# Attention's first score steps placed between the last second layers of an expert stage, and the end of the kernel re-ordered

## The reference, cut to what matters

```
x = x + conv(norm(x))        # a long convolution over time, done with a Fourier transform
x = x + experts(norm(x))     # 8 experts, the best 2 of each token weighed by a softmax
x = x + attention(norm(x))   # 16 heads of 8 features, 4 sets of queries, causal softmax
x = x + experts(norm(x))     # the same 8 experts again
```

## Time and profile before

| | us |
|---|---|
| median of 3 runs | 831.67 |
| the three runs | 830.97, 831.67, 833.51 |
| the profiled execution's own time | 832.0 |
| its span | 830.3 |
| busy: PE, PEld | 778.1, 425.8 |
| busy: ACT, DVE, POOL | 717.3, 641.0, 552.9 |
| granted TensorE clock, mean | 0.994 of full |

### The profile page before, as it was taken

How to read it: one execution, slowest core, us unless ns; L and a number is a source line. 1 busy time by engine, 2 the same in 40 slices (tenths; PEclk the granted TensorE clock), 3 DMA queues, 4 the chain that set the end, 5 groups by cost and what they waited for, 6 DMA issues and landing times.

```text
span 830.3 us, 20345 instructions
## 1 busy us (share of the span) xinstructions
PE 778.1 (94%) x7697; PEld 425.8 (51%) x7697; DVE 641.0 (77%) x1914; ACT 717.3 (86%) x917; POOL 552.9 (67%) x610
## 2 busy tenths in 40 slices
PE   3898999999999899999999999999999999999995
PEld 1444766766667333333333333333334677777774
DVE  6896899977897656776776776777555999888884
ACT  4623988988988999999999999999998799999983
POOL 2785566455534889888888888889886454454442
PEclk9999999999999999999999999999999999999998
DMA  9211000000023234443433433334400000000000
GB/s 292 82 51 52 2 1 2 2 2 1 2 55 96 62 97 102 103 98 83 101 89 88 96 100 81 87 103 102 103 1 2 2 14 15 15 13 16 13 15 17
DMA packets 38521, 46.87 MB, mean 56 GB/s; under 512 B 6185, under 2 KB 23858, under 8 KB 38418
## 3 DMA queue, kind: packets, MB, share of 16 engines
q1 hardware_dynamic: 38418, 45.51, 20.9%
HBM read 28.71 MB, written 16.78 MB: 55 GB/s over the span
## 4 chain that ended last, share of the span: by engine, by line
PE 57%; ACT 13%; DVE 10%; POOL 8%; issue 8%; ACTq 0%; POOLq 0%; DVEq 0%
PE psum L944 16%; PE psum L890 14%; PE psum L1242 12%; ACT prob L1200 10%; PE psum L1191 5%; PE psum L1300 4%; DVE mixed L956 3%; POOL prob L1215 3%; DVE hidden_parts_first L913 2%; PE psum L674 2%; PE psum L1084 1%; PE psum L766 1%; POOL prob L1212 1%; POOL prob L1210 1%; POOL rstd L367 1%
## 5 line engine op out<-in xcount | busy, mean ns | idle before, releaser
L1200 ACT ACTIVATE prob<-psum 128x1536 f32<-128x1536 f32 x256 | 347.4, 1500 | 15.5 <-PE psum L1191 15.5
L1242 PE MATMUL psum<-prob,vstack 128*32 128x256 f32 (+1 forms) x2048 | 204.9, 495 | 1.6 <-DVE o_tok L1250 1.6
L890 PE MATMUL psum<-xt_parts,w_parts 128*128 128x512 f16 x768 | 186.6, 379 | 0.0
L956 DVE SCALAR_TENSOR_TENSOR mixed<-psum,comb_y,mixed 128x128 f32<-128x128 f32 x512 | 143.2, 340 | 2.1 <-PE psum L944 2.1
L920 POOL TENSOR_TENSOR hidden_parts_second<-hidden_second,hidden_parts_second 128x512 f16<-128x512 f32 x64 | 77.4, 1209 | 94.4 <-ACT hidden_parts_second L906 94.3
L920 POOL TENSOR_TENSOR hidden_parts_first<-hidden_first,hidden_parts_first 128x512 f16<-128x512 f32 x64 | 76.7, 1201 | 73.4 <-ACT hidden_parts_first L906 73.1
L1210 POOL TENSOR_SCALAR_AFFINE_SELECT prob<-prob 128x512 f32<-128x512 f32 x128 | 84.2, 658 | 44.5 <-ACT prob L1200 39.1
L1191 PE MATMUL psum<-qstack,kstack 32*128 32x512 f16 x768 | 99.6, 384 | 9.6 <-POOL prob L1215 4.8
L1191 PEld LDWEIGHTS psum<-qstack,kstack 32*128 32x128 f16 x768 | 24.8, 91 | 158.1 <-ACT prob L1200 139.6
L904 ACT ACTIVATE hidden_second<-psum,b 128x512 f32<-128x512 f32 x128 | 88.3, 690 | 20.2 <-PE psum L890 16.5
L890 PEld LDWEIGHTS psum<-xt_parts,w_parts 128*128 128x128 f16 x768 | 72.0, 99 | 64.3 <-issue 1.4
(11 more groups left out here) (137 smaller groups left out, 1018.1 us busy)
## 6 DMA issues: line engine op xcount, KB each, us to landing
qstack<-qk_parts SPq DMA_DIRECT2D x128, 128.0 KB, 3.6
qk_parts<-parts SPq DMA_DIRECT2D x64, 192.0 KB, 3.1
kstack<-qk_parts SPq DMA_DIRECT2D x128, 32.0 KB, 3.5
stream<-L_attn_a_u SPq DMA_DIRECT2D x4, 512.0 KB, 8.2
kept_x<-stream SPq DMA_DIRECT2D x4, 512.0 KB, 2.7
out<-mixed SPq DMA_DIRECT2D x8, 256.0 KB, 2.3
mirror<-u_mirror SPq DMA_DIRECT2D x4, 256.0 KB, 7.2
w_whole<-L_ffn_W SPq DMA_DIRECT2D x1, 1024.0 KB, 8.6
```

The source lines that it names most:

```text
L890: last = e.matmul(bank(u % 4), m.w1[:, w_part, ex, cols], xt_parts[:, s, x_part, :], start=(n == 0), stop=(n == len(PRODUCTS) - 1))
L956: last = e.scalar_tensor_tensor(out=m.y[:, t0 + t, :], in0=bank(down_bank(m, i))[:, t * P:(t + 1) * P], scalar=comb_y[:, s, t, ex:ex + 1], ...
L1200: e.activation(prob[:, n % PROBS, :], psum[:, TILE * (n % 2):TILE * (n % 2 + 1)], ACT.Exp, scale=SCALE)\
L1242: last = e.matmul(to[SLOT * lane:SLOT * (lane + 1)], vstack[:, b % 2, keys, first:first + SLOT], weights_of(n - t, lane, keys, pair), star ...
```

## The change

In the first expert stage the last two second layers get banks 6 and 7 in place of 4 and 7 (6 only after `lo_done` 6, the last low part of batch 1's queries and keys). Scores 0 move ahead of the second layer of unit 62 and wait for one relu less; scores 1 move between the second layers of 62 and 63 and wait for all relus and the accumulation of unit 61; scores 2 follow the second layer of 63, ahead of `tensor_at_x(2)`, which now waits for the accumulation of unit 62 instead of `lo_done` 6. In the last unit of the second stage each tile gets a bank of its own (0 to 3) and a release of its own, and VectorE adds tile by tile; the last chunk is stored in two transfers of 128 KB, the first after two tiles. The load of `bad` (`verdict`) stands ahead of the wait for the last accumulation, on SyncE ahead of the last stores; only SyncE waits for the stores, the other engines wait for them only inside the general version.

```
     def down_bank(m, i):
-        return 7 if m is first and i == EXPERTS * FFN_CHUNKS - 1 else 4 + i % 2
+        ahead = i - (EXPERTS * FFN_CHUNKS - LAG)
+        return 6 + ahead if m is first and ahead >= 0 else 4 + i % 2
+
+    def is_last(m, ch, ex):
+        return m is second and (ch, ex) == (FFN_CHUNKS - 1, EXPERTS - 1)
+
+    def down_place(m, ch, ex, t):
+        if is_last(m, ch, ex):
+            return bank(t)[:, 0:P]
+        return bank(down_bank(m, (m.at + ch) * EXPERTS + ex))[:, t * P:(t + 1) * P]
...
-        if i >= 2:
+        if i >= 2 and not is_last(m, ch, ex):
             e.wait_ge(accum, i - 1)
-        if down_bank(m, i) == 7:
+        if down_bank(m, i) == 6:
+            e.wait_ge(lo_done, 6)
+        elif down_bank(m, i) == 7:
             e.wait_ge(based, FFN_CHUNKS)
         for t in range(FFN_TILES):
             for n, (h_, w_) in enumerate(terms):
-                last = e.matmul(to[:, t * P:(t + 1) * P], h_[:, t * P:(t + 1) * P], w_, start=(n == 0),
+                last = e.matmul(down_place(m, ch, ex, t), h_[:, t * P:(t + 1) * P], w_, start=(n == 0),
                                 stop=(n == len(terms) - 1))
+            if is_last(m, ch, ex) and t + 1 < FFN_TILES:
+                last.then_inc(last_down, 1)
         last.then_inc(down_up, 1)
...
         for t in range(FFN_TILES):
+            if is_last(m, ch, ex) and t + 1 < FFN_TILES:
+                e.wait_ge(last_down, t + 1)
+            elif is_last(m, ch, ex):
+                e.wait_ge(down_up, i + 1)
             last = e.scalar_tensor_tensor(out=m.y[:, t0 + t, :], in0=down_place(m, ch, ex, t), ...
+            if is_last(m, ch, ex) and t + 1 < FFN_TILES:
+                last.then_inc(last_accum, 1)
         last.then_inc(accum, 1)
...
@@ tensor_at_x
         elif b == 2:
-            e.wait_ge(lo_done, 6)
+            e.wait_ge(accum, EXPERTS * FFN_CHUNKS - 1)
@@ tensor_scores
         elif n == 1:
-            e.wait_ge(accum, EXPERTS * FFN_CHUNKS - 1)
+            e.wait_ge(relued, HBLK * EXPERTS * FFN_CHUNKS)
+            e.wait_ge(accum, EXPERTS * FFN_CHUNKS - LAG)
         else:
-            e.wait_ge(relued, HBLK * EXPERTS * FFN_CHUNKS)
+            e.wait_ge(relued, HBLK * EXPERTS * FFN_CHUNKS - 1)
@@ tensor_first
+        tensor_scores(e, 0)
         tensor_down(e, first, *TAIL[0])
-        tensor_scores(e, 0)
+        tensor_scores(e, 1)
         tensor_down(e, first, *TAIL[1])
+        tensor_scores(e, 2)
@@ tensor_attention
-            if n:
+            if n > 2:
                 tensor_scores(e, n)
...
+    STORED = 16 * (FFN_CHUNKS + 1)
+
+    def sync_store_last(e):
+        for t in range(0, FFN_TILES, FFN_TILES // 2):
+            if t == 0:
+                e.wait_ge(last_accum, FFN_TILES // 2)
+            else:
+                e.wait_ge(accum, 2 * EXPERTS * FFN_CHUNKS)
+            at = slice(TILES - FFN_TILES + t, TILES - FFN_TILES // 2 + t)
+            e.dma_start(out_tiles[:, at, :], mixed[:, at, :]).then_inc(s_stored, 16)
...
-    def unless_good(e, body):
+    def verdict(e):
+        e.wait_ge(judged, 2)
+        return e.value_load(bad[0:1, 0:1], min_val=0, max_val=1)
+
+    def unless_good(e, body, found):
         e.wait_ge(accum, MAIN)
-        e.wait_ge(judged, 2)
-        e.wait_ge(s_stored, 16 * FFN_CHUNKS)
-        with e.If(e.value_load(bad[0:1, 0:1], min_val=0, max_val=1)):
+        with e.If(found):
+            e.wait_ge(s_stored, STORED)
             body(e)
...
@@ sync_program
-        for ch in range(FFN_CHUNKS):
+        for ch in range(FFN_CHUNKS - 1):
             sync_store(e, second, ch, s_stored)
-        unless_good(e, sync_general)
+        found = verdict(e)
+        sync_store_last(e)
+        e.wait_ge(s_stored, STORED)
+        unless_good(e, sync_general, found)
@@ the four other engines' programs, as here on TensorE
-        unless_good(e, tensor_general)
+        unless_good(e, tensor_general, verdict(e))
```

More of the change, by code:

```diff
@@ L306, in build_in @@
     combt_up, combt_copied, base_up, based = (sem(n) for n in ("comb_t_up", "comb_t_copied", "base_up", "based"))
+    last_down, last_accum = sem("last_expert_down"), sem("last_expert_accumulated")
     hid_up, relued, low_first, low_second, down_up, accum = (sem(n) for n in (
@@ L923, in down_bank @@
     def down_bank(m, i):
-        return 7 if m is first and i == EXPERTS * FFN_CHUNKS - 1 else 4 + i % 2
+        ahead = i - (EXPERTS * FFN_CHUNKS - LAG)
[6 more added lines that the diff above has]
+        return bank(down_bank(m, (m.at + ch) * EXPERTS + ex))[:, t * P:(t + 1) * P]
     def tensor_down(e, m, ch, ex):
         i = (m.at + ch) * EXPERTS + ex
-        r, to = i % HRING, bank(down_bank(m, i))
+        r = i % HRING
         if m.whole:
@@ L949, in vector_accumulate @@
         s, i, t0 = ch % 2, (m.at + ch) * EXPERTS + ex, ch * FFN_TILES
-        e.wait_ge(down_up, i + 1)
+        if not is_last(m, ch, ex):
+            e.wait_ge(down_up, i + 1)
         if ex == 0:
@@ L955, in vector_accumulate @@
         for t in range(FFN_TILES):
-            last = e.scalar_tensor_tensor(out=m.y[:, t0 + t, :], in0=bank(down_bank(m, i))[:, t * P:(t + 1) * P],
+            if is_last(m, ch, ex) and t + 1 < FFN_TILES:
+                e.wait_ge(last_down, t + 1)
+            elif is_last(m, ch, ex):
+                e.wait_ge(down_up, i + 1)
+            last = e.scalar_tensor_tensor(out=m.y[:, t0 + t, :], in0=down_place(m, ch, ex, t),
                                           scalar=comb_y[:, s, t, ex:ex + 1], in1=m.y[:, t0 + t, :], op0=ALU.mult,
                                           op1=ALU.add)
+            if is_last(m, ch, ex) and t + 1 < FFN_TILES:
+                last.then_inc(last_accum, 1)
         last.then_inc(accum, 1)
@@ L1858, in sync_general @@
             sync_store(e, gen_second, ch, s_stored)
-        e.wait_ge(s_stored, 2 * 16 * FFN_CHUNKS)
+        e.wait_ge(s_stored, STORED + 16 * FFN_CHUNKS)
     def tensor_general(e):
@@ L2000, in gpsimd_program @@
         gpsimd_second(e)
-        unless_good(e, gpsimd_general)
+        unless_good(e, gpsimd_general, verdict(e))
     def scalar_program(e):
@@ L2010, in scalar_program @@
         scalar_second(e)
-        unless_good(e, scalar_general)
+        unless_good(e, scalar_general, verdict(e))
     def vector_program(e):
@@ L2018, in vector_program @@
         vector_second(e)
-        unless_good(e, vector_general)
+        unless_good(e, vector_general, verdict(e))
     def tensor_program(e):
```

## The result

The changed kernel takes 828.87 us (median of 9 runs, 827.53 to 831.3), the kernel before 831.97 us (9 runs, 830.97 to 833.51). The ratio is 0.9964, 95% interval 0.9952 to 0.9977: faster by 0.36%, or 3.0 us (1.9 to 4.0). The prediction had 827.0 us, a gain of 4.7 on the 831.67 that it knew. The profiled execution took 830.0 us with a span of 828.3.

A forecast was written before the change was run, and what follows sets the result against it. ScalarE and TensorE bound attention and TensorE the second expert stage, so gains come only at the seam and the end. Seam 1.5 plus tail 3.2 (3.4 less 0.2) gives 4.7 us off 831.67: 827.0, own range 825.6 to 828.2.

The forecast's parts named there:

- the range to 829.2: Whole kernel: the forecast's range widened to take in the first two rivals almost whole, leaving out about 0.15 of chance.
- the second rival: Program's end: the tail gives half, some 2.0 us, through TensorE's fetch holding the store or a long SyncE fetch; 828.2, chance 0.14.
- three signs of being wrong: Gaps between attention's exp groups grow; the last store lands over 2.0 us after issue; TensorE still resumes last.
- Seam: Entry into attention: earlier scores start exp 2 at 272.0 instead of 273.58, and attention keeps the shift; gain 1.5 us.
- the seam gives nothing: Entry into attention: something unshifted starts attention's cycle, so only the tail's gain is left; 828.5 us, chance 0.10.
- the longer rhythm in each batch: Attention: VectorE's late copy for batch 2 brings longer gaps, 0.5 us lost in each of 15 batches; 834.5 us, chance 0.03.
- Tile by tile: Last unit: only the last addition remains after TensorE's last matmul, ending at 821.67 instead of 822.45; gain 0.8 us.
- Two stores: Last chunk's store: the first half goes out early, so half the packets remain after the second issue; gain 0.5 us.
- SyncE's end in place of TensorE's: Program's end: SyncE ends last, with 3.0 us behind its branch in place of TensorE's 4.2; gain 1.2 us.
- The fetches beside the last store: Program's end: other engines' code fetches run beside the store's packets; cost between 0 and 1.45 us, taken as 0.2.
- The verdict ahead: Program's end: loading the flag before the last stores removes load and register work between landing and branch; gain 0.9 us.
- the end's four terms: Program's end: 0.8 (additions), 0.5 (halved store), 0.9 (early flag) and 1.2 (SyncE last), together 3.4 us.

The follow-up runs named there:

- e1: The kernel before with only the seam's edits, its end left as before; 830.44 us, ratio to the kernel before 0.9980.
- e10: The changed kernel with the last unit in one bank with one release, both halves stored after the last addition; 830.01 us, ratio to the kernel before 0.9971.
- e3: The changed kernel, but all engines wait for the landed stores ahead of their branches; 828.99 us, ratio to the kernel before 0.9958.
- e5: The changed kernel, but TensorE too waits for the landed stores ahead of its branch; 828.72 us, ratio to the kernel before 0.9964.
- e6: The changed kernel, but ScalarE, VectorE and GpSimd too wait for the landed stores ahead of their branches; 829.98 us, ratio to the kernel before 0.9970.
- e4: The changed kernel, but SyncE branches right after issuing the last store and waits for the landing behind the branch; 826.58 us, ratio to the kernel before 0.9929.
- e9: The changed kernel with the flag loaded behind the waits again on all engines; 827.56 us, ratio to the kernel before 0.9940.
- e8: e4 with the wait for the last accumulation also moved into the general version; 825.83 us, ratio to the kernel before 0.9930.
- e2: The changed kernel with the seam's edits taken back, only the end changed; 830.72 us, ratio to the kernel before 0.9982.
- e7: The changed kernel with the last chunk stored by one 256 KB transfer after the last addition; 829.36 us, ratio to the kernel before 0.9965.

## Why the prediction was right or wrong

The direction held, and both gains are there. But the size was too large, 4.7 us for 3.0, and 828.87 lies outside the forecast's own range (825.6 to 828.2). It is inside the range to 829.2 only because that was widened for the rivals, and what happened at the end is what the second rival describes. Of the three signs of being wrong one came true: the last store landed 3.4 us after its issue, over the 2.0 set there. By its steps:

- **Seam, 1.5 predicted, 1.25 to 1.28 measured.** The starts of exp 0, 1 and 2 were to be 268.8, 270.3 and 272.0; they are 268.74, 270.50 and 272.33. The missing time lies where TensorE goes from second layers to score steps and back: 0.12 us at the first, 0.04 and 0.07 at the two pairs behind it, which I left out because the row of the kernel before had only one such place. That the cycle of attention carries the offset whole is shown (e1). VectorE's copy for batch 2 starts at 272.98, as predicted (272.95), and costs nothing. The rival "the seam gives nothing" is refuted, and so is the longer rhythm in each batch: up to the clock dip the gaps are the same to 0.01 us.
- **Tile by tile, 0.8 predicted, 0.77 in the trace,** and e10's trace gives it back. Right for the path; the total doesn't resolve it.
- **Two stores, 0.5 predicted.** Right in a kernel that fetches no code meanwhile (1.8 against 2.3); in the changed one not resolved.
- **SyncE's end in place of TensorE's, 1.2 predicted.** Right, and more: SyncE resumes 2.7 us behind its branch, 0.3 less than I took. But TensorE is back 2.5 us before it, not 0.2, because the late landing holds only SyncE.
- **The fetches beside the last store, a loss of 0.2 predicted with a bound of 1.45.** This is the step that failed: "I take 0.2, near the q14 blocks, because TensorE's block comes at about 823.0, when most packets are through." The loss is 3.4 - 1.8 = 1.6 us (e3), of which TensorE's block has 1.1 or more (e5, e6). The reason given fails twice. The block came at 822.8, 0.9 us behind TensorE's branch, and 276 of 544 packets had moved by then, hardly any of the second half. And in e4, where 516 had moved, the landing took 4.4 us all the same: a store is landed when its last packet is, and 16, by their count those of one transfer engine, stood behind the block. The upper bound, 1.45, was the right one to take, and even it was a little low, since the 16 packets behind the block went slower too.
- **The verdict ahead, 0.9 predicted.** Its saving on SyncE is real (e9 pays 0.9 us from landing to branch), but it was not the whole of its effect: it also moved TensorE's branch onto the store. e9, which takes it back, is faster. I had priced each part at the place where it acts and this one has two.

With these corrections the sum is 1.25 (seam) + 3.4 (the end's four terms as predicted) + 0.3 (SyncE faster) - 1.6 = 3.35 us, against 3.0 in the ratio and 3.4 from the traces. The second rival, "the tail gives half", had this mechanism and the time 828.2; its chance of 0.14 looks too small.

The rule from the Trainium skill's page "Runtime: NRT & Kernel Launch" (Instruction fetch mechanics), that a taken branch outside the window stalls for a fetch, agreed throughout: in e8, where TensorE branched 0.7 us and ScalarE 4.3 us earlier against the last second layer, ScalarE and TensorE still needed 2.6 and 3.8 us each, only at a time when nobody waited. The figure of the Trainium skill's page "DMA: Bandwidth & Descriptors" (Anatomy of one DMA), some 2.0 us fixed for a transfer, which that section gives for transfers issued from GpSimd, is close but not a floor for those of SyncE: 1.8 us were enough for 128 KB from issue to landing (e3, e9).

## What to carry to other kernels

A branch over much code cost 2.5 to 4.8 us on every engine here that had such code, and the time counts only where it ends last. Take it as early as the engine's own work allows, beside the last store and not behind it, and let only what stands inside the rarely taken side wait for the rest. When an early step starts traffic on shared transfer engines, price the last packet of the transfer that ends the program, not the mean.

## What the runs showed of the hardware that was not expected

- One block of code of 16 KB on a transfer queue made a 128 KB store land 1.1 to 1.7 us later, two of 8 KB up to 0.5 us (e3, e5, e6), although the three together (32 KB) are an eighth of the bytes of the last chunk (256 KB). 16 packets of the store, by their count those of one transfer engine, moved after the block, at 61 ns each instead of 27.
- SyncE resumed 2.5 to 2.8 us behind its branch when ScalarE and VectorE had branched 1.6 us or more before (changed kernel, e2, e5, e7, e9, e10; in e5 TensorE branched with it), and 3.0 to 3.7 us behind it when these two branched with it (before, e1, e3, e6); with VectorE alone it was 3.1 (e8). So engines that fetch at the same time can slow each other.
- The granted clock of TensorE was 0.66 of full for 5 us late in attention in one execution (changed kernel) and 1.00 in another with the same instructions there (e4), with TensorE busy all of that stretch in both. It cost 1.4 us, about half of what the whole change brings, and is a reason to compare parts by a stretch of the trace and kernels by many runs.
